# Layer 0 in 196 steps of 512 columns that run through all images, with three image buffers

## The reference

```python
p2 = x[:, :, _I2] * x[:, :, _J2]
y2 = jnp.einsum('bgihw,goi->bgohw', p2, W2).reshape(B, Ch, H, Wd) + b2[None, :, None, None]
p3 = x[:, :, _I3] * x[:, :, _J3] * x[:, :, _K3]
y3 = jnp.einsum('bgihw,goi->bgohw', p3, W3).reshape(B, Ch, H, Wd) + b3[None, :, None, None]
return inp + y2 * beta2 + y3 * beta3 * CONV3_SCALE
```

## Time and profile before

| | us |
|---|---|
| time, median of 3 runs (5242.01 to 5245.78) | 5245.67 |
| profiled execution | 5247.06 |
| its span | 5245.2 |
| first TH transfers issued (image 0 closed) | 41.57 |
| last TH transfers issued (image 31 closed) | 739.58 |

### The profile page before, as it was taken

How to read it: one execution, slowest core, us unless ns; L and a number is a source line. 1 busy time by engine, 2 the same in 40 slices (tenths; PEclk the granted TensorE clock), 3 DMA queues, 4 the chain that set the end, 5 groups by cost and what they waited for, 6 DMA issues and landing times.

```text
span 5245.2 us, 89835 instructions
## 1 busy us (share of the span) xinstructions
PE 5209.2 (99%) x32798; PEld 2560.9 (49%) x32798; DVE 4419.9 (84%) x8971; ACT 5103.2 (97%) x3032; POOL 4427.4 (84%) x1854
## 2 busy tenths in 40 slices
PE   9999999999999999999999999999999999999999
PEld 4444455444545454445454444545454544444544
DVE  8888888888888888888888888888888888888887
ACT  7888889999999999999999999999999999999998
POOL 6666655898888998888999898899888899888988
PEclk9999999999999999999999999999999999999999
DMA  7888751222222222233222222232222322222122
GB/s 161 166 178 166 164 109 38 57 59 59 61 54 55 62 63 63 63 63 63 60 59 47 52 62 61 57 65 58 48 63 63 63 63 63 63 63 55 43 42 48
DMA packets 227284, 380.57 MB, mean 73 GB/s; under 512 B 158181, under 2 KB 175390, under 8 KB 216734
## 3 DMA queue, kind: packets, MB, share of 16 engines
q1 hardware_dynamic: 225728, 373.82, 34.2%
q10 hardware_dynamic: 1118, 1.00, 0.1%
HBM read 259.08 MB, written 102.74 MB: 69 GB/s over the span
## 4 chain that ended last, share of the span: by engine, by line
PE 75%; ACT 14%; issue 7%; DVE 2%; SPq 1%; DMA 0%; POOL 0%; DVEq 0%; POOLq 0%
PE at_AV L1260 32%; PE at_S L1219 19%; ACT at_ring L1003 10%; PE at_AV L1266 10%; PE l_TY L583 6%; ACT at_ring L1009 4%; PE l_TY L590 3%; PE l_SEL L572 3%; PE at_AV L1256 2%; DVE at_ring L1076 1%; SPq L436 0%; DMA l_TH<-l_YO 0%; DVE at_GT L1136 0%; PE at_AV L1231 0%; DVE l_U L540 0%
## 5 line engine op out<-in xcount | busy, mean ns | idle before, releaser
L1076 DVE TENSOR_SCALAR_CACHE_REDUCE at_ring<-at_S 128x1344 f32<-128x1344 f32 (+2 forms) x2352 | 2882.6, 1242 | 460.2 <-PE at_S L1219 443.5
L953 POOL TENSOR_TENSOR at_ZP<-at_ZP,at_ring 128x1568 f32<-128x1568 f32 x640 | 2263.8, 3572 | 146.4 <-ACT at_ring L1009 136.4
L1260 PE MATMUL at_AV<-at_ring,at_GT 128*64 128x392 f32 x12800 | 2300.2, 500 | 4.6 <-issue 3.6
L1003 ACT ACTIVATE at_ring<-at_ring,at_NM 128x3136 f32<-128x3136 f32 x784 | 2277.1, 2905 | 12.1 <-DVE at_NM L1085 10.9
L1009 ACT ACTIVATE at_ring<-at_ring,at_RZ 128x3136 f32<-128x3136 f32 x784 | 2278.4, 2906 | 0.0
L1260 PEld LDWEIGHTS at_AV<-at_ring,at_GT 128*64 128x64 f32 x12800 | 853.9, 137 | 1144.9 <-issue 1106.9
L1219 PE MATMUL at_S<-at_THM,at_THS 128*128 128x448 f32 x5376 | 1381.6, 387 | 11.0 <-DVE at_ring L1076 8.6
L1219 PEld LDWEIGHTS at_S<-at_THM,at_THS 128*128 128x128 f32 x5376 | 927.0, 188 | 630.7 <-DVE at_ring L1076 291.8
L974 POOL TENSOR_TENSOR at_OUTB<-at_OUTB,at_ZB 128x1568 f32<-128x1568 f32 x246 | 877.8, 3568 | 16.8
L1266 PE MATMUL at_AV<-at_ring,at_ones 128*32 128x392 f32 x7168 | 677.1, 498 | 2.9 <-DVE at_ACC L1169 2.9
L540 DVE TENSOR_TENSOR l_U<-l_TY,l_XB 128x448 f32<-128x448 f32 x896 | 496.7, 616 | 90.9 <-PE l_TY L583 88.3
(11 more groups left out here) (86 smaller groups left out, 2522.2 us busy)
## 6 DMA issues: line engine op xcount, KB each, us to landing
at_THM<-hld SPq DMA_DIRECT2D x128, 392.0 KB, 6.8
at_THS<-hld SPq DMA_DIRECT2D x256, 192.0 KB, 4.1
l_X<-in_x SPq DMA_DIRECT2D x124, 392.0 KB, 7.6
at_CIN<-att SPq DMA_DIRECT2D x62, 406.0 KB, 7.6
at_ZB<-rzd SPq DMA_DIRECT2D x62, 406.0 KB, 7.6
yd<-l_YO SPq DMA_DIRECT2D x128, 196.0 KB, 5.4
att<-at_ACC SPq DMA_DIRECT2D x248, 98.0 KB
at_OUTB<-yd SPq DMA_DIRECT2D x62, 392.0 KB, 8.4
```

Source lines behind the costliest of these rows:

```text
L953: e.tensor_tensor(z, z, v, ALU.add).then_inc(g_add, 1)
L1003: e.activation(v, v, ACT.Exp, bias=NM[:, i:i + 1], accum_out=ZS[:, i:i + 1]).then_inc(a_p1, 1)
L1076: e.tensor_scalar(ring[:, s % RING, SC * a_:SC * b].rearrange("p (b w) -> p b w", w=SC), PS[:, k % 2, bank:bank + b - a_, 0:SC], 1.0, None ...
L1260: ins = e.matmul(dst[64 * j:64 * j + 64, 0:QC], GT[fl.n % 2][:, keys_of(fl.n, t), :], ring[:, slot, q:q + QC], start=(i == 0), stop=(i == ...
```

## The change

A step is CH = 512 columns and steps run on through the images as if all 32 x 3136 columns were one row; NU = 32 x 3136 / 512 = 196. Eight images are 49 steps. `pieces(u)` gives the one or two stretches of images that step u covers: (image, first column, end, place in the step). masked, parts and close run once for each piece, PE and ACT work on the whole step. The semaphores of masked and parts count pieces, that of close counts steps. `last_step(n)` is the step that holds the last column of image n: 6, 12, 18, 24, 30, 36, 42, 48, 55, ... X2 has three buffers, and load(n + NX) waits until the pieces of image n have been read. The split of image n comes after parts(last_step(n) + 5). The first loads of image 0 are cut at 512 and 1536 columns (before at 448 and 1344). All tiles of a step become 512 columns wide.

```diff
-NCH = 7
-NX = 4
-CH = HW // NCH
+CH = 512
+NX = 3
-SPLIT_AT = 12
+SPLIT_LATE = 5
+def pieces(u):
+    c = CH * u
+    n, lo = divmod(c, HW)
+    hi = min(lo + CH, HW)
+    first = [(n, lo, hi, 0)]
+    return first if hi - lo == CH else first + [(n + 1, 0, CH - hi + lo, hi - lo)]
+def pieces_to(u):
+    return sum(len(pieces(i)) for i in range(u + 1))
+def last_step(n):
+    return (HW * (n + 1) - 1) // CH
+def read_to(n):
+    return pieces_to(last_step(n)) - (len(pieces(last_step(n))) - 1)
...
-    NU = NCH * n_img
+    NU = HW * n_img // CH
...
         def load(n):
             if n >= NX:
-                e.wait_ge(g_x, NCH * (n - NX + 1))
+                e.wait_ge(g_x, read_to(n - NX))
...
-            e.wait_ge(v_t, y_use(NCH * n + NCH - 1) + 1)
+            e.wait_ge(v_t, y_use(last_step(n)) + 1)
...
         def masked(u):
-            n = u // NCH
-            if u in (0, 1):
-                e.wait_ge(s_l0[u], 64)
-            elif u % NCH == (3 if n == 0 else 0):
-                e.wait_ge(s_ld[n % NX], 64 * (n // NX + 1))
             if u >= 2:
-                e.wait_ge(g_x, u - 1)
-            e.tensor_scalar(XH[u % 2][:, :], X2[n % NX][:, cols(u)], vec[:, 1:2], 0.0, ALU.mult, ALU.add)\
-             .then_inc(g_m, 1)
+                e.wait_ge(g_x, pieces_to(u - 2))
+            for n, lo, hi, at in pieces(u):
+                if u in (0, 1):
+                    e.wait_ge(s_l0[u], 64)
+                elif lo == 0 or u == 3:
+                    e.wait_ge(s_ld[n % NX], 64 * (n // NX + 1))
+                e.tensor_scalar(XH[u % 2][:, at:at + hi - lo], X2[n % NX][:, lo:hi], vec[:, 1:2], 0.0, ALU.mult, ALU.add)\
+                 .then_inc(g_m, 1)
 
         def parts(u):
-            e.wait_ge(g_m, u + 1)
+            e.wait_ge(g_m, pieces_to(u))
             if u >= 4:
                 e.wait_ge(p_sel, 3 * (u - 3))
-            e.tensor_tensor(XX[u % 4][:, :], X2[(u // NCH) % NX][:, cols(u)], XH[u % 2][:, :].bitcast(F32),
-                            ALU.subtract).then_inc(g_x, 1)
+            for n, lo, hi, at in pieces(u):
+                w = slice(at, at + hi - lo)
+                e.tensor_tensor(XX[u % 4][:, w], X2[n % NX][:, lo:hi], XH[u % 2][:, w].bitcast(F32),
+                                ALU.subtract).then_inc(g_x, 1)
...
-            n, r = divmod(u - SPLIT_AT, NCH)
-            if r == 0 and n >= 0:
+            for n in range(n_img):
+                if u == last_step(n) + SPLIT_LATE:
+                    split(n)
+        for n in range(n_img):
+            if NU <= last_step(n) + SPLIT_LATE:
                 split(n)
...
         def close(u):
-            n = u // NCH
             e.wait_ge(p_y, u + 1)
-            if u % NCH == 0 and n >= 2:
-                e.wait_ge(s_st[n % 2], 64 * (n // 2))
-                e.wait_ge(s_th, 128 * (n - 1))
-            e.tensor_scalar(YO[n % 2][:, cols(u)], TY[y_use(u) % 4][:, 0:CH], bt[:, 0:1], None, ALU.add)\
-             .then_inc(v_t, 1)
+            for n, lo, hi, at in pieces(u):
+                if lo == 0 and n >= 2:
+                    e.wait_ge(s_st[n % 2], 64 * (n // 2))
+                    e.wait_ge(s_th, 128 * (n - 1))
+                ins = e.tensor_scalar(YO[n % 2][:, lo:hi], TY[y_use(u) % 4][:, at:at + hi - lo], bt[:, 0:1], None, ALU.add)
+            ins.then_inc(v_t, 1)
...
             if s == 0:
-                e.wait_ge(g_x, u + 1)
+                e.wait_ge(g_x, pieces_to(u))
```

More of the change, by code:

```diff
@@ L375, in y_use @@
         return 4 * min(u + 2, NU) + u
-    def cols(u):
-        return slice((u % NCH) * CH, (u % NCH + 1) * CH)
     def stored(e):
@@ L487, in gpsimd @@
                 parts(u)
-            n, r = divmod(u - SPLIT_AT, NCH)
-            if r == 0 and n >= 0:
+            for n in range(n_img):
[3 more added lines that the diff above has]
+            if NU <= last_step(n) + SPLIT_LATE:
                 split(n)
-        for n in range(max(0, (NU - 1 - SPLIT_AT) // NCH + 1), n_img):
-            split(n)
     def scalar(e, roots):
@@ L558, in vector @@
                 fold(u - FOLD_AT)
-        e.wait_ge(g_x, NU)
+        e.wait_ge(g_x, pieces_to(NU - 1))
         ahead_of_last()
```

## The result

| | before | after |
|---|---|---|
| time, median of 4 runs each, us | 5244.96 | 5298.14 |
| profiled execution, us | 5247.06 | 5297.93 |
| its span, us | 5245.2 | 5296.1 |
| first TH transfers issued, us | 41.57 | 42.94 |
| last TH transfers issued (image 31 closed), us | 739.58 | 791.58 |

The ratio is 1.0100, with a 95% interval from 1.0083 to 1.0118: slower by 53 us, where 48 were forecast. All of it is in layer 0: from the last TH transfers to the end of the span are 4505.6 us before and 4504.5 after.

The account below looks back on a forecast made before the run. The prediction took TensorE (PE) to set layer 0's pace: -11.2 us from fewer, longer steps, +61.4 from 31 stalls behind the early split, -2.6 for old stalls, sum +47.6, so 5294 us; range 5266 to 5330.

Parts of the forecast that it names:

- The sum: All terms, all in layer 0: -11.2 us for steps, +61.4 for stalls, -2.6 for old stalls, together +47.6 us.
- Steps: Layer 0: 196 steps of 3.60 us in place of 224 of 3.20, -11.2 us.
- The bound by the column, 3.657: Layer 0 steps: if all cost goes by column, a step takes 3.20 x 8/7 = 3.657 us and nothing is gained.
- The place of the split: POOL's split comes a step earlier, leaving 9.71 us for a chain of 11.69 us; PE stands, +61.4 us.
- The size of the stall: PE waiting for POOL's XX after the early split: 1.98 us an image, 31 times; bounds 1.29 and 2.56.
- issue to cast: From SP starting the TH transfers to POOL's cast behind their landing: 6.8 us, the median before.
- Second pieces: Steps across image borders: 28 have one more masked, parts and close; free except 0.12 us each in the chain.
- Three buffers: Image loads with three buffers: POOL waits some 1.3 us in its own idle time; hidden by 4 us, cost 0.
- Half clock: Rival: PE's clock halves after some or all stalls in layer 0, 5300 to 5340 us; chance 0.25.
- No stall: Rival: POOL is released in time and PE never waits, leaving -11.2 - 2.6, so 5233 us; chance 0.12.
- half a stall: Rival: landings all 6.52 us and an earlier close, PE waits 0.5 to 1.2 us an image, 5250 to 5275; chance 0.08.
- late image: Rival: load(n+3) lands over 4 us later than now and PE waits for it, 5320 us and above; chance 0.05.

Follow-up runs that it names:

- experiment 8: The kernel before with eight steps of 392 columns an image and the split after parts(L + 7), L being the image's last step: 5256.31 us, ratio 1.0021.
- experiments 1 and 2: First, late6: changed kernel, split one step later, 5233.75 us; second, b_at11: kernel before, split one step earlier, 5358.28 us.
- late6: The changed kernel with the split one step later, after parts(last step + 6), nothing else different: 5233.75 us, ratio 0.9979 to the kernel before.
- experiment 3: The kernel before with three image buffers in place of four, nothing else: 5246.68 us, ratio 1.0004.
- experiment 5: The changed kernel, split still early, with four of the eight TH transfers left out: 5233.70 us, ratio 0.9978 to the kernel before.
- b_at11: The kernel before with its split one step earlier, after parts(last step + 5), still 448 columns and four buffers: 5358.28 us, ratio 1.0217.
- late4: The changed kernel with the split yet a step earlier, after parts(last step + 4): 5469.71 us, ratio 1.0428 to the kernel before.

## Why the prediction was right, point by point

**The sum.** 53 us measured, 48 forecast, and the mechanism is the one forecast. That the two are so near is in part luck: the gain from the steps is 2 us smaller, the stalls are 4 us shorter, and 6 us of clock stood in no term of the sum.

**Steps.** 3.61 us, 3.60 forecast; -9.2 us for -11.2. The bound by the column, 3.657, would have been 9 us more in the layer and is out; experiment 8 says the same.

**The place of the split.** Right, and experiments 1 and 2 show it from both sides: put back, the loss is gone; put into the old kernel, the loss is there. The issue point of TH was forecast at 1.09 us behind the select and is there.

**The size of the stall.** 1.98 us forecast; 57.5 / 31 = 1.85 measured. Its terms: issue to cast, 6.8 forecast, has a mean of 6.82 but a median of 6.56, because it is at its floor, 6.52 to 6.6, in most images and 7.0 to 7.7 in ten. At the floor TH issue to TH issue is 23.34 us, that is a stall of 1.68; by the prediction's sum with 6.53 for the landing it would be 1.71.

**Second pieces.** The border of image 15, which lies on a step border and has no second piece, comes 23.12 us after the one before it, the others at the floor 23.34: 0.22 for the two pieces (`close` and `parts`), for which 0.12 + 0.12 were put. Outside the chain they cost nothing: late6 has them, and PE waits for POOL only once, 0.9 us.

**Three buffers.** Hidden as forecast, and by experiment 3 at no cost. POOL waited for an image 27.7 us in 18 waits (1.5 each, 1.3 forecast). With the stall gone there is less cover: in late6 77.5 us in 26 waits, the longest 4.2, still without cost.

**Half clock.** The rival had a chance of a quarter, and it was there in part, too little for its time (5315 if under half of the stalls are followed by a slow stretch). Three of the 31 images had one. Their rows in the stage table, with an undisturbed image as the last:

```profile
42.90:68.60 25.70, 23.43 (x136) 9.16 (x132) 19.14 (x32) 18.90 (x19) 14.70 (x16) 0.93 0.62 111
283.80:309.70 25.90, 23.35 (x136) 8.75 (x132) 19.17 (x32) 18.87 (x19) 14.84 (x17) 0.93 0.82 168
309.70:337.10 27.40, 24.62 (x136) 9.41 (x132) 19.17 (x32) 18.92 (x19) 14.65 (x16) 0.88 0.67 136
163.70:187.00 23.30, 21.69 (x136) 8.44 (x132) 19.44 (x32) 18.80 (x19) 14.46 (x16) 1.00 0.77 155
```

(1 - 0.93) x 25.7 + (1 - 0.93) x 25.9 + (1 - 0.88) x 27.4 = 6.9 us of clock, 88% of it columns, so 6 us, an estimate. The forecast took all stalls as alike. They weren't, and only long ones were followed by a slow stretch: two borders in a row, where the products (L607) behind the first take 1.91 us and those behind the second 1.02:

```profile
322.32 0.80 PE L596 MATMUL l_SEL<-l_XX,l_sel 64*128 64x512 f32 x2 [2.78 <-POOL l_XX L491]
322.92 1.91 PE L607 MATMUL l_TY<-l_P,l_WT 64*128 64x512 f32 x4
...
349.68 0.50 PE L596 MATMUL l_SEL<-l_XX,l_sel 64*128 64x512 f32 x2 [2.80 <-POOL l_XX L491]
350.01 1.02 PE L607 MATMUL l_TY<-l_P,l_WT 64*128 64x512 f32 x4
```

Nine of the 31 stalls last 2.27 to 2.80 us; three of them (2.27, 2.55, 2.78) have a slow stretch behind them. The other 22, up to 2.1 us, have none.

**No stall, half a stall, late image.** None came. The point named for the first, a landing under 4.8 us, was tried by experiment 5: at 4.03 the kernel is the 5233 that this case gave.

## What to carry to other kernels

Where an engine waits in its queue for a transfer, count the steps between the event that starts the transfer and the first result from behind the wait that the bound engine needs. One step less there cost the bound engine the whole shortfall every time, though the engine that waited was busy for only two thirds of the time. When the step or tile size of a pipeline changes, work these distances out again in microseconds: the constant that was right in one unit (u = 12) is not right as another (last step + 5).

## What the runs showed that I had not expected

How steeply the clock's cost comes in. In the changed kernel PE stands once an image, after otherwise dense work, for 1.9 us in the mean: 3 of 31 images had a slow stretch. In b_at11 it stands for 2.3 to 3.4 us, 2.6 in the mean: 20 of 31 had one, by the granted clock of the trace, and the loss is 113 us where the waits are 81. In late4 it stands for 4.9 to 6.8: all of them, with some 2.1 us each on top of the stall. The Trainium skill's "TensorE: Matmul & The Clock Gate", Part 1, has the direction (too little activity halves the clock), and the trace agrees. So in these kernels a stall of 1.6 us cost only itself, and one of 2.3 or more brought, often but not always, some 1.6 us besides. The length of the stall alone doesn't decide it: 2.80 us left the clock whole and 2.27 didn't.

The fixed part of a step was the same at 392, 448 and 512 columns to within 0.01 us. And a faster layer had later landings: with the stall gone, the mean from TH issue to cast rose from 6.82 to 7.13 us, up to 9.6. Perhaps the same transfers are more crowded in less time (from 43 to 728 us the DMA share is 0.76 in the change and 0.81 in late6), but no run tries this alone. The reserve of late6, 2 us over the floor, covers nearly all of it: in the whole layer PE waits for POOL once, for 0.9 us.
